# The gathers of the experts' rows: four tasks of two on GpSimd, ranked below its sums, in place of one task of eight

## What is computed

```python
x = _layernorm(x + _L0_attn_ref(x, ...))            # a state space mixer, 1024 channels x 16 states, and a gated MLP
x = _layernorm(x + _L0_xattn_ref(ctx_1024, x, ...)) # a second mixer on the context, 512 channels x 16 states, gated by x
x = _layernorm(x + _L0_ffn_ref(x, ...))             # 2 of 8 experts for each token, and a shared MLP
x = _layernorm(x + _L1_attn_ref(x, ...))            # attention in segments of 4
x = _layernorm(x + _L1_xattn_ref(x, ctx_1024, ...)) # mixing of rows by a softmax over the context
x = _layernorm(x + _L1_ffn_ref(x, ...))             # a softmax over 64, top 8, and biases by them
```

```python
topk_w, topk_idx = jax.lax.top_k(scores, K)          # K = 2
expert_out = jnp.einsum('tef,ehf->teh', g, w_down)
y = jnp.einsum('te,teh->th', cw, expert_out)         # cw: the weights of a token's two experts, else 0
```

## Time and profile before

| | us |
|---|---|
| median of 3 runs | 3151.66 (3150.8 to 3157.52) |
| the profiled execution | 3149.89 |
| its span, first to last instruction | 3147.8 |
| VectorE busy | 2461.9 |
| PE busy | 2395.0 |
| ScalarE busy | 1234.9 |
| GpSimd busy | 1054.0 |

### The profile page before, as it was taken

One profiled execution on the slowest core, in us unless ns is written; L12 is line 12 of the kernel. 1 busy time (PEld: TensorE's weight loads), 2 busy tenths in 40 slices (PEclk: granted clock), 3 DMA queues, 4 the chain that ended last, 5 costly groups with the idle time before them and its releaser, 6 DMA issues.

```text
span 3147.8 us, 20459 instructions
## 1 busy us (share of the span) xinstructions
PE 2395.0 (76%) x6316; PEld 1147.8 (36%) x6316; DVE 2461.9 (78%) x1928; ACT 1234.9 (39%) x1970; POOL 1054.0 (33%) x291
## 2 busy tenths in 40 slices
PE   5687899228969876689688875896887838969965
PEld 1243333103424443334344433343443324445532
DVE  5997997998979998899799889897998993121132
ACT  4434454424353452552434534524345332021222
POOL 0342233354434445424344454244444530000000
PEclk7887999558979998699889987898899869979986
DMA  2125552202212764022116740221265502216920
GB/s 78 34 100 167 177 180 69 102 0 85 64 37 86 221 225 138 25 95 66 41 64 222 236 148 25 87 67 40 76 199 186 173 0 81 77 44 225 297 65 14
DMA packets 156573, 339.60 MB, mean 108 GB/s; under 512 B 30448, under 2 KB 47856, under 8 KB 151792
## 3 DMA queue, kind: packets, MB, share of 16 engines
q1 hardware_dynamic: 130864, 261.41, 26.4%
q10 hardware_dynamic: 20480, 60.10, 5.2%
q0 software_dynamic: 5120, 16.78, 1.6%
HBM read 296.16 MB, written 57.54 MB: 112 GB/s over the span
## 4 chain that ended last, share of the span: by engine, by line
PE 38%; DVE 32%; issue 14%; ACT 8%; POOL 3%; DMA 3%; ACTq 0%; SPq 0%; DVEq 0%; POOLq 0%
DVE hb L1523 12%; PE ps L719 6%; PE ps L902 6%; PE ps L764 5%; PE ps L909 5%; DVE hb L1531 4%; DVE hb L1436 4%; POOL ya L1802 2%; DMA ring<-in_w_edn 2%; PE ps L1036 2%; PE ps L945 2%; PE ps L832 2%; PE ps L875 1%; DVE sm L1379 1%; ACT T L1318 1%
## 5 line engine op out<-in xcount | busy, mean ns | idle before, releaser
L1802 POOL TENSOR_TENSOR ya<-ya,hb 128x2048 f32<-128x2048 f32 x188 | 857.6, 4562 | 1383.0 <-DVE hb L1523 1326.5
L1523 DVE TENSOR_TENSOR_SCAN hb<-da,hb 128x2048 f32<-128x2048 f32 x192 | 858.5, 4471 | 2.3 <-ACT da L1076 0.7
L1076 ACT ACTIVATE da<-dl,pk 128x511 f32<-128x511 f32 x768 | 489.3, 710 | 453.8 <-DVE hb L1523 445.7
L1436 DVE TENSOR_TENSOR hb<-du,ps 128x2048 f32<-128x2048 f32 x192 | 436.1, 2271 | 35.0 <-POOL ya L1802 26.1
L1531 DVE TENSOR_TENSOR hb<-hb,ps 128x2048 f32<-128x2048 f32 x192 | 437.6, 2279 | 3.6 <-PE ps L849 2.9
L764 PE MATMUL ps<-V,ring 128*128 128x512 f32 x512 | 237.7, 620 | 30.7 <-DVE V L1464 18.1
L729 PE MATMUL ps<-bct,sel 64*128 64x512 f32 x192 | 106.3, 554 | 191.5 <-DVE hb L1436 181.9
L719 PE MATMUL ps<-ring,hid 128*128 128x512 f32 x544 | 246.8, 610 | 3.8 <-DVE hid L1568 3.1
L926 PE MATMUL ps<-ring,hid 128*128 128x352 f32 x480 | 194.9, 489 | 14.4 <-ACT hid L1289 7.9
L930 PE MATMUL ps<-ring,hid 128*128 128x352 f32 x480 | 190.2, 479 | 13.0 <-ACT X L1306 12.9
L902 PE MATMUL ps<-T,ring 128*128 128x512 f32 x352 | 167.6, 621 | 28.7 <-DVE T L1556 19.4
(11 more groups left out here) (265 smaller groups left out, 3324.8 us busy)
## 6 DMA issues: line engine op xcount, KB each, us to landing
ring<-egu SPq DMA_DIRECT2D x240, 352.0 KB, 3.9
ring<-in_w_edn SPq DMA_DIRECT2D x72, 512.0 KB, 5.5
ring<-in_w_fgu SPq DMA_DIRECT2D x44, 512.0 KB, 3.7
ring<-in_w_in SPq DMA_DIRECT2D x32, 512.0 KB, 4.0
hid<-xrows SPq DMA_DIRECT2D x60, 256.0 KB, 4.4
yrows<-X ACTq DMA_DIRECT2D x60, 256.0 KB, 4.6
ring<-in_w_egu SPq DMA_DIRECT2D x24, 512.0 KB, 3.3
ring<-in_w_edn SPq DMA_DIRECT2D x60, 192.0 KB, 4.4
```

What stands on the lines that cost most here:

```text
L1076: i = act.activation(dav(n % 2)[:, k, 1:], dl[:, k, 1:], ACT.Exp, scale=Aneg[:, (4 * (u % 3 - 1) if u % 3 else UC) + k, m:m + 1])
L1436: dve.tensor_tensor(hbv(m % NHB), du[:, :, :], wide(ps[:, 5, :], 4), ALU.mult).then_inc(s["dbu"], 1)
L1523: dve.tensor_tensor_scan(hb[:, h, :], da[:, b % 2, :], hb[:, h, :], 0.0, ALU.mult, ALU.add)\
L1802: pool.tensor_tensor(sums, ya[:, :, :], hbv(m % NHB), ALU.add).then_inc(s["acc"], 1)
```

## The change

The one task `gath` of a sequence becomes four, `gath` 0 to 3, with two indirect DMAs each. Each has a guessed length of 3.4 us (the one task had 8) and the rank 45 (it had 30), which puts it behind a sum, at 40, that could start as early. Each follows the one before; `comb` waits for the last. The waits for the experts' results stand in front of the first task alone. The DMAs themselves, their number and their order, stay.

```diff
-            put(30, ("gath", b, 0), "pool", 8, (("bd", b, 2 * NBLK - 1), "act", 4))
+            for g in range(TT):
+                put(45, ("gath", b, g), "pool", 3.4, (("bd", b, 2 * NBLK - 1), "act", 4), (("gath", b, g - 1), "pool") if g else None)
...
-        put(30, ("comb", b, 0), "dve", 5.7, at, (("gath", b, 0), "pool", 4))
+        put(30, ("comb", b, 0), "dve", 5.7, at, (("gath", b, TT - 1), "pool", 3))
...
                     elif t == "gath":
-                        pool.wait_ge(*of("ye_b", b, NBLK))
-                        pool.wait_ge(s["yst0"], 16 * (b + 1) * ((NBLK + 1) // 2))
-                        pool.wait_ge(s["yst1"], 16 * (b + 1) * (NBLK // 2))
-                        for k, name in enumerate(("gath0", "gath1")):
-                            for e in range(TT):
-                                o = k * TT + e
-                                pool.indirect_dma_start(hid[:, 6 + e, :] if k else X[:, e, :], None, yrows,
-                                                        bass.IndirectOffsetOnAxis(ap=posu[:, o:o + 1], axis=0))\
-                                    .then_inc(s[name], 16)
+                        if n == 0:
+                            pool.wait_ge(*of("ye_b", b, NBLK))
+                            pool.wait_ge(s["yst0"], 16 * (b + 1) * ((NBLK + 1) // 2))
+                            pool.wait_ge(s["yst1"], 16 * (b + 1) * (NBLK // 2))
+                        for o in (2 * n, 2 * n + 1):
+                            k, e = divmod(o, TT)
+                            pool.indirect_dma_start(hid[:, 6 + e, :] if k else X[:, e, :], None, yrows,
+                                                    bass.IndirectOffsetOnAxis(ap=posu[:, o:o + 1], axis=0))\
+                                .then_inc(s[f"gath{k}"], 16)
```

## The result

The changed kernel takes 3157.36 us (median of 13 runs, 3154.11 to 3165.02), the kernel before, run beside it, 3152.15 (13 runs, 3148.87 to 3161.18). The ratio is 1.0018, with an interval of 1.0009 to 1.0026: 5.7 us slower (2.8 to 8.2). The forecast was 3.1 us faster. The time lies within the range of 3138 to 3160, but on the other side of no change.

The account below looks back on a forecast made before the run. Bound: VectorE's scan and GpSimd's sum alternating, 8.9 us a step. Sequences 0 and 1 lose 9.8 us (points 1 to 5), point 6 wins 8.8, point 7 4.1: 3.1 us less, 3148.5 us, range 3138 to 3160.

Parts of the forecast that it names:

- Point 1: Sequences 0 and 1, product behind the gathers: waits 4.6 us for 9.1, a scan shutting the sum out; 4.5 less each.
- Point 2: Sequences 0 and 1, adding of gathered rows: stalled by a GpSimd sum running beside it; 4.5 us more each.
- Point 3: Sequences 0 and 1, segment scores: moved from behind the products to behind a scan; 2.7 us more each.
- Point 4: Sequences 0 and 1, turn to the next unit: PE alternates cross mixes with step-size matmuls; 1.6 us more each.
- Point 5: Sequences 0 and 1, from the turn to the next sequence's first scans: ScalarE's exponentials delay; 0.6 us more each.
- Point 6: Norm and gate stage: earlier norm frees the next unit sooner; 6 us less in sequence 2, 2.8 in sequence 1.
- Point 7: Sequence 2: gathers one sum earlier, 1.8 us less; fewer stalls in the attention rows, 2.3 us less.
- slower, by sums out in the open: Rival: sequences 0 and 1 lose 9.4 us each, get back 4.5; 3157.4 if the gate stage doesn't pay; chance 0.21.
- the likeliest case: Whole kernel: small changes either way, 3145.4 to 3158 us, holding the forecast's 3.1 us gain; chance 0.5.

Follow-up runs that it names:

- e12: e4 with, on VectorE alone in sequences 0 and 1, one scan moved ahead of the adding and the norm 2 statistics; 1.0024 of the kernel before.
- e15: e4 with, on VectorE alone in sequences 0 and 1, the segment scores and their scaling moved behind scan 92 (140); 1.0045 of the kernel before.
- e6: Changed kernel with the mix stretch of sequences 0 and 1 back in the old order on VectorE, PE and ScalarE; 1.0050 of the kernel before.
- e10: Changed kernel with the adding and the bias and feed-forward stretches of sequences 0 and 1 back in the old order; 1.0003 of the kernel before.
- e7: Changed kernel with the bias and feed-forward stretch of sequences 0 and 1 back in the old order; 1.0017 of the kernel before.
- after: The changed kernel itself, with split gathers and the planner's new order on four engines, against the kernel before; 3157.36 us, ratio 1.0018.
- e9: Changed kernel with the adding and mix stretches of sequences 0 and 1 back in the old order; 0.9973 of the kernel before.
- e4: Changed kernel with the old order on all engines up to scan 154, but gathers of sequences 0 and 1 kept split; 0.9968 of the kernel before.
- e3: Changed kernel with the old order on all engines up to scan 154, gathers of sequences 0 and 1 unsplit; 0.9984 of the kernel before.
- e2: Changed kernel with only GpSimd's gathers of sequences 0 and 1 back in one row of eight; 1.0053 of the kernel before.

## Why the prediction was wrong, point by point

- **Point 1, the wait behind the gathers (-4.5 per sequence): right in size, wrong in form.** The sum isn't shut out by the scan, it shuts the scan out (9.12 us). The prediction took it for shown that a scan keeps a sum out; but in the kernel before the sums wait at a semaphore for a scan's end (1326.5 of 1383.0 us), so its trace could not show it. Within the new order the split is worth 4.2 us, in the old order 2.35, as the rows then come late. I had not costed that.
- **Point 2, the adding stalled (+4.5): the stall was right, 7.25 for 2.73 us. The price was not.** The step "I take 4.5" counted the stalled instructions and not who waits for them. Alone (e12, where 2.1 us of waiting for rows go) it is 7 us in the profile, 8.9 by the medians.
- **Point 3, the segment scores (+2.7): the stall right again** (L1694: 3.12 us as median of its four, for 0.69), and again more by itself (8.4 in e15's profile). In the changed kernel both moves together cost 4.3 us net by scan 94, since each covers the other's wait.
- **Point 4, the turn (+1.6): can't be priced alone.** The new order saves 10 us in both sequences together if the adding is late (e6); if it isn't, the stretch itself costs 2.5 and 1.6 us, and all of e10 11.0.
- **Point 5, the bias stage (+0.6): mis-sized on the way, right at the end.** It loses 6 us on VectorE by scan 100, and they don't reach PE's stretch: 0.3 us between e7 and after, 1.6 between e9 and e4.
- **Point 6, the gate stage (-2.8 and -6.0): this step failed, and with it the sign.** In sequence 2 I let the norm run at S to S + 3.0, S being the last scan's end. The matmuls of the residual end 5.5 us behind S when VectorE is in time (e3). The earlier trace rows had them 7.7 behind it, 5.42 of waiting and one product of 2.29; moving the residual ahead of one short row won about 2 us and not the whole. The step sizes, forecast at S + 23.3, begin at S + 30.6 in e3; in after, where VectorE comes late and finds PE done, they begin at S + 24.5, so the rest of the chain was nearly right. Measured: 1.3 us lost (e3, e4) for 6.0 won. In sequence 1 the third wait did go, but the norm's last small operation stood under a sum, and ScalarE did the norm ahead of its fourth eviction. VectorE waited 15.13 us for the step sizes where before it waited 9.92, and they began at S + 24.5 for a forecast of S + 21.1; 0.7 us lost for 2.8 won. Two rows of after, VectorE:

```profile
1540.89 3.18 DVE L1387 TENSOR_SCALAR mv<-mv 128x4 f32<-128x4 f32 x1
1559.21 2.29 DVE L1505 SCALAR_TENSOR_TENSOR hb<-hb,da 128x2048 f32<-128x2048 f32 x1 [15.13 <-ACT da L1249]
```

- **Point 7, sequence 2's gathers and attention rows (-4.1): right.** From scan 161 to 191 4.3 us in after, 5.1 in e3. The attention rows take 13.1 us for 15.0 (forecast 12.7).

The forecast's sum for sequences 0 and 1 was +7.0 us (with point 6's share). Measured, the split is -4.4 and the order +15.8, +11.4 in all; with the order taken first (e2 against e3) it is +21.7 and the split -11.0, so the two can't be priced apart. Sequence 2 was -10.1 and is -5.0. The rival "slower, by sums out in the open", at 3157.4 with point 6 not paying, named the outcome. That the median meets this number to 0.1 us is luck: its parts, +9.8 and -4.1, were +11.4 and -5.0. Its condition, ScalarE behind, isn't what happened in sequence 2, where PE was. I gave it too little, since the term that kept the likeliest case on the fast side had no row for PE's end, only for VectorE's wait.

What isn't settled: 0.7 us between the last scan and the end of after's span, how often PE's clock takes its 2.7 us in front of scan 128, and whether the medians of e12 and e15, 2 us per sequence above their profiles, hold more than noise.

## What to carry to other kernels

Price a moved step by its first late successor, not by its own stall: follow the chain until a wait in the profile is long enough to absorb the delay. Before booking a gain at a stage, ask which engine ends it; here an interval where PE runs almost without gaps both ate VectorE's gains and forgave its losses. Before comparing two profiles, compare PE's granted clock stretch by stretch. When a planner's small change reorders four engines, splice old and new order lists: the wanted edit (here the split, 10.1 us with sequence 2's part) may be good and its company bad, and pieces of one plan belong together.

## What the runs showed of the hardware that was not expected

- A GpSimd sum recorded 0.29 us after the scan's start (1228.43 and 1228.14) still went first: 4.53 us for the sum, 9.12 for the scan. The same pair, the sum recorded 0.27 to 0.30 us behind the scan and the scan taking 9.1 us, stands in sequences 0 and 1 of every run with split gathers. The order of recorded starts doesn't tell who is held.
- Issues of indirect DMAs are held by scans as the earlier trace rows showed, again 4.91 and 4.44 us for 0.95.
- Small VectorE instructions with all operands in SBUF wait out a sum too: L1387, 128x4, 3.18 us for 0.17; in e4's timeline L1653, 128x32, 4.39 us for 0.19:

```profile
2226.78 4.39 DVE L1653 TENSOR_TENSOR hid<-hid,sm 128x32 f32<-128x32 f32 x1
```

The Trainium skill (SBUF — State Buffer, Who interferes with whom) states that issue order decides who blocks. For the pair above the record's starts would name the scan as the first, and it was the one held, so by recorded starts this trace doesn't bear the rule out. The same section has `tensor_scalar` among the operations with modes that take the shared pair, which fits L1387.
